# Per-batch feed-forward weights W1 + M1 and W2 + M2 formed in SBUF a turn ahead, in place of correction matmuls in every turn

## The reference

```
lt   = x[:, 1:17];  even, odd = lt[:, ::2], lt[:, 1::2]
m1   = (even[:, :4, :, None] * odd[:, :4, None, :]).reshape(B, 1024, 256)
m2   = (even[:, 4:, :, None] * odd[:, 4:, None, :]).reshape(B, 256, 1024)
h    = gelu(x @ W1.T + scale * x @ m1.T + b1)
out  = h @ W2.T + scale * h @ m2.T + b2
```

## Time and profile before

| | |
|---|---|
| median of three runs | 1988.76 us (1985.94 to 1989.46) |
| profiled execution | 1991.09 us, span 1989.3 us |
| mean granted TensorE clock | 0.995 |
| busy | PE 97%, DVE 69%, ACT 56%, POOL 20% |
| first half, turns 1 to 15 | 63.9 us a turn |
| second half, looped turns | 56.1 us a turn |

### The profile page before, as it was taken

The page is one execution under the profiler, slowest core; times in us unless marked ns, Lnnn a source line. Parts: engine busy times, 40 slices in busy tenths (PEclk is TensorE's granted clock), DMA queues, the critical chain, the costliest instruction groups (busy, mean ns, idle before and its releaser), DMA issues.

```text
span 1989.3 us, 41475 instructions
## 1 busy us (share of the span) xinstructions
PE 1927.2 (97%) x14078; PEld 1803.2 (91%) x14078; DVE 1367.9 (69%) x3408; ACT 1115.5 (56%) x2334; POOL 407.1 (20%) x650
## 2 busy tenths in 40 slices
PE   7999999999999999999987899999999999999998
PEld 6788888888888888888886899999999999999998
DVE  7877776776777776776746566766666666766665
ACT  5655565555655565555655655554555555544553
POOL 2222222222222222222213511111111101111100
PEclk9999999999999999999999999999999999999999
DMA  4000000000000000000012200000000000000000
GB/s 162 12 22 21 11 11 21 21 21 5 16 21 21 11 11 21 21 21 6 10 34 89 67 15 15 12 17 17 11 16 16 17 12 17 12 17 12 17 7 12
DMA packets 47211, 44.51 MB, mean 22 GB/s; under 512 B 6848, under 2 KB 45376, under 8 KB 47168
## 3 DMA queue, kind: packets, MB, share of 16 engines
q1 hardware_dynamic: 47168, 43.96, 6.9%
HBM read 34.77 MB, written 8.39 MB: 22 GB/s over the span
## 4 chain that ended last, share of the span: by engine, by line
PE 83%; DVE 7%; ACT 5%; issue 3%; POOL 1%; SPq 1%; DMA 0%; DVEq 0%; ACTq 0%; POOLq 0%
PE ring L618 9%; PE ring L620 9%; PE ring L619 9%; PE ring L1820 7%; PE ring L1818 7%; PE ring L1819 7%; PE ring L671 4%; PE sim L1818 3%; PE sim L1819 3%; PE sim L1820 3%; PE sim L618 3%; PE sim L620 2%; PE sim L619 2%; PE ps_x L1818 2%; PE ps_x L1820 2%
## 5 line engine op out<-in xcount | busy, mean ns | idle before, releaser
L411 ACT ACTIVATE a_pr<-sim,a_nmax 128x512 f32<-128x512 f32 x256 | 174.5, 689 | 208.4 <-DVE a_nmax L537 208.3
L1818 PE MATMUL ring<-b_xch,b_weh 128*128 128x256 f32 x1024 | 289.5, 283 | 1.7 <-DVE b_act_e L1464 1.7
L1819 PE MATMUL ring<-b_xcl,b_weh 128*128 128x256 f32 x1024 | 285.7, 279 | 0.0
L1820 PE MATMUL ring<-b_xch,b_wel 128*128 128x256 f32 x1024 | 285.6, 279 | 0.0
L326 POOL TENSOR_SCALAR a_pr<-a_pr,a_rinv 128x512 f32<-128x512 f32 x256 | 183.1, 729 | 498.3 <-DVE a_rinv L547 495.4
L1818 PEld LDWEIGHTS ring<-b_xch,b_weh 128*128 128x128 f32 x1024 | 192.3, 188 | 1.9 <-DVE b_act_e L1464 1.9
L1819 PEld LDWEIGHTS ring<-b_xcl,b_weh 128*128 128x128 f32 x1024 | 193.0, 188 | 0.0
L1820 PEld LDWEIGHTS ring<-b_xch,b_wel 128*128 128x128 f32 x1024 | 192.1, 188 | 0.0
L1464 DVE TENSOR_TENSOR b_act_e<-b_act_e,ring 128x512 f32<-128x512 f32 x128 | 87.9, 687 | 116.7 <-PE ring L1820 102.4
L528 DVE TENSOR_TENSOR a_ptl<-ring,a_pth 128x512 fp32r<-128x512 f32 x256 | 163.9, 682 | 3.1 <-ACT a_pth L401 2.0
L515 DVE SCALAR_TENSOR_TENSOR a_ktl<-ring,a_bkv_s,a_kth 128x512 fp32r<-128x512 f32 x128 | 95.3, 744 | 102.1 <-ACT a_kth L391 102.1
(11 more groups left out here) (378 smaller groups left out, 6246.0 us busy)
## 6 DMA issues: line engine op xcount, KB each, us to landing
a_c_in<-in_ctx_in SPq DMA_DIRECT2D x16, 256.0 KB, 2.6
a_x_in<-in_x SPq DMA_DIRECT2D x16, 256.0 KB, 2.9
a_x_res<-in_x SPq DMA_DIRECT2D x16, 256.0 KB, 2.6
x_between<-a_x_out SPq DMA_DIRECT2D x16, 256.0 KB, 2.2
b_x_s<-x_between SPq DMA_DIRECT2D x16, 256.0 KB, 2.6
b_up<-b_ev SPq DMA_DIRECT2D x256, 1.0 KB
out_x<-b_acc SPq DMA_DIRECT2D x16, 256.0 KB, 2.2
b_ct_raw<-in_ctxT SPq DMA_DIRECT2D x15, 256.0 KB, 2.6
```

Source lines behind the costliest of these rows:

```text
L411: nc.scalar.activation(pr[:, h % 2, t, :], sim[t][:], ACT.Exp, bias=nmax[:, h % 2, t:t + 1], accum_out=rsum[:, h % 2, t:t + 1]).then_inc(e ...
L1818: nc.tensor.matmul(out, lh, rh, start=(n == 0), stop=False)
L1819: nc.tensor.matmul(out, lh, rl, start=False, stop=False)
L1820: last = nc.tensor.matmul(out, ll, rh, start=False, stop=(n == len(parts) - 1 and not more))
```

## The change

The corrections are gone. Instead the weights themselves are made for every item, one turn ahead. The item's first 32 rows of `x1` are loaded a second time, normalized apart (`rows_stats`, `rows_rstd`, `rows_apply`), written to DRAM (`rows_between`) and read back in two forms: the eight even rows broadcast to all partitions (`even_b`, 8 KB in each partition) and the odd rows turned (`odd_raw`, single 4-byte elements), by `rows_spread`. ScalarE then writes each rank-one product into the raw weight tiles (`update`, 16 instructions of 128x256 a turn), two accumulating DMAs for each of W1 and W2 (`weights_added`, issued by GpSimd) add the weights from DRAM to them, ScalarE writes the high halves (`weight_high`, eight of 128x512) and GpSimd the low halves (`weight_low`, eight of 128x512). For items 0 and 1 the products are made by GpSimd, in turns 14 and 15 of the first half; turn 14 is written out of the loop for that (`ahead`). The split of W1 and W2 in turn 0 and their load at the start are gone.

Two other things are moved. In each turn the chain's fills stand earlier beside the experts' on TensorE, with VectorE and ScalarE ordered to match. In the warm turn the low halves of experts 4 to 7 go from GpSimd to VectorE.

```diff
+        def rows_spread(n):
+            take(rows_ready, n + 1)
+            sp.dma_start(z_t[n], first_rows[1:1 + 4 * NL, :]).then_inc(rows_out, 16)
+            take(rows_out, n * 16 + 16)
...
+            sp.dma_start(even_b[:], z_two[n, 0].unsqueeze(0).to_broadcast([P, 2 * NL, D])).then_inc(spread_in, 16)
+            for c in range(DC):
+                sp.dma_start(odd_raw[:, c, :], z_two[n, 1][:, c * P:(c + 1) * P].rearrange("r p -> p r"),
+                             allow_slow_non_contiguous=True).then_inc(spread_in, 16)
...
+        def weights_added(n, w):
+            take(w_made[w], n * 4 + 4)
...
+            for c in (slice(0, half), slice(half, 2 * half)):
+                pool.dma_start(dst[:, c], src[:, c], accum_op=ALU.add).then_inc(w_in[w], 16)
+
+        def weight_low(n, w, q):
+            take(w_hi[w], n * 4 + q + 1)
+            raw, high, low = (w_piece(w, q, tile) for tile in W[w])
+            nc.gpsimd.tensor_tensor(low, raw, f32(high), ALU.subtract).then_inc(w_lo[w], 1)
...
     def scalar(act):
+        def update(n, w, q):
+            act.wait_ge(odd_ready, n + 1)
...
+            for k in range(2):
+                part, row, by = rank_one(w, q, k)
+                last = nc.scalar.activation(part, row, ACT.Copy, scale=by)
+            last.then_inc(w_made[w], 1)
+
+        def weight_high(n, w, q):
+            act.wait_ge(w_in[w], n * 32 + 32)
+            raw, high, _ = (w_piece(w, q, tile) for tile in W[w])
+            nc.scalar.activation(high, raw, ACT.Copy).then_inc(w_hi[w], 1)
...
     def tensor(pe):
-                last = nc.tensor.matmul(cd[:, k, :], up1[:, n, k * P:(k + 1) * P], zm[:], start=False, stop=True)
...
                 if chain:
                     pe.wait_ge(lo["A"], t + 1)
-                    pe.wait_ge(lo["Z"], t + 1)
-                    pe.wait_ge(up_in, (t + 1) * UPS * 16)
+                    pe.wait_ge(w_lo["1"], t * 4 + 4)
```

More of the change, by code:

```diff
@@ L296, in turn @@
                 other.early(0)
+            if is_ahead(b):
+                other.ahead(0)
         sections_of(sp, turn)
@@ L357, in turn @@
                     other.early(h)
+                if is_ahead(b):
+                    other.ahead(h)
         sections_of(pool, turn)
@@ L1006, in rest, with turn @@
             sp.sem_inc(out_done, 16)
-            def turn(t, chain, more, warm):
+            def turn(t, chain, more, more2, warm):
+                if more2:
+                    rows_load(t + 2)
                 if more:
@@ L1323, in rest, with turn, experts @@
         def rest():
-            def turn(t, chain, more, warm):
+            def turn(t, chain, more, more2, warm):
                 i = t - 1
-                for e in warm_in(0) if warm else ():
-                    for j in range(3):
-                        expert_high(e, j)
+                def experts(slot):
+                    for e in warm_in(slot) if warm else ():
+                        for j in range(3):
+                            expert_high(e, j)
+                experts(0)
                 silu(i, 1)
@@ L1335, in turn @@
                     gelu_high(t, 1)
-                for e in warm_in(1) if warm else ():
-                    for j in range(3):
-                        expert_high(e, j)
                 if chain:
@@ L1361, in turn @@
-                silu(i, 4)
+                if chain:
+                    copy_high(t, "V", hh[:, V, 0:S])
+                experts(3)
+                if more:
+                    update(t + 1, "1", 2)
                 if chain:
                     copy_high(t, "B", xth[:])
-                    copy_high(t, "V", hh[:, V, 0:S])
+                if more:
+                    update(t + 1, "1", 3)
+                silu(i, 4)
                 hidden_high(i, 4)
-                for e in warm_in(4) if warm else ():
-                    for j in range(3):
-                        expert_high(e, j)
@@ L1396, in turn @@
                     hidden_high(t, 0)
+                if more:
+                    weight_high(t + 1, "2", 2)
+                    weight_high(t + 1, "2", 3)
+                if chain:
                     tanh_high(t)
             sections_of(act, turn)
-        return Beside(early, beside, rest)
+        return Beside(early, ahead, beside, rest)
     def vector(dve):
@@ L1724, in beside, with turn @@
                 distances(0)
+                for q in range(4):
+                    weight_low(1, "2", q)
         def rest():
-            def turn(t, chain, more, warm):
+            def turn(t, chain, more, more2, warm):
                 i = t - 1
@@ L1767, in turn @@
                     norm_apply(t + 1, "A", x1_s)
-                hidden_low(i, 4)
-                weigh(i, 3)
-                if chain:
-                    queries_low(t)
-                hidden(i, 5)
                 if chain:
                     maxima(t)
+                if warm:
+                    for j in range(3):
+                        expert_low(6, j)
+                hidden(i, 5)
                 hidden_low(i, 5)
-                if more:
-                    even_low(t + 1)
                 if chain:
@@ L1819, in product @@
                 nc.tensor.matmul(out, lh, rl, start=False, stop=False)
-                last = nc.tensor.matmul(out, ll, rh, start=False, stop=(n == len(parts) - 1 and not more))
+                last = nc.tensor.matmul(out, ll, rh, start=False, stop=(n == len(parts) - 1))
             return last
```

533 lines of the change are left out of this document (273 added, 260 removed).

## The result

The changed kernel took 2112.32 us (median of four, 2110.63 to 2114.19), the kernel before 1988.72 beside it: ratio 1.062, 95% interval 1.061 to 1.064. The forecast was 1954, with a range to 1998.

The account below looks back on a forecast made before the run. TensorE, busy 97% of the span, was taken as the bound. Net 1.34 us a turn over 14 turns (18.8 us) + 3 + 8 - 1.5 + 7 gave 35 us: 1954 on the median's scale, range 1934 to 1998.

Parts of the forecast that it names:

- What goes from TensorE: Looped turn: update matmuls, narrower `y_fill`, Z, W2 update and G's transposes go, 2.25 us; with B's wait 2.79 us.
- the wait at B: Looped turn, TensorE ahead of B's transposes: the 0.54 us wait goes, as `second_residual` no longer waits for the correction.
- Beside C: Turn's end: C's transposes come before `down` 6, leaving the C chain less time; 0.25 us allowed, bounds 0 and 0.8.
- the GpSimd step: Looped turn: eight low halves on GpSimd, 11.1 us, both weights in time by about 4 and 8 us.
- rival D: Turn's end: GpSimd's low halves lock out an expert's low half, about 1 us a turn, 14 us, 1968; chance 0.12.
- The step on the accumulating DMAs: Looped turn: W1's transfers hidden; W2's land about 10 us after issue, up to 12 allowed: hidden, narrowly.
- The new wait ahead of `y_fill`: Looped turn: two W2 high halves ahead of the tanh delay ScalarE 1.06 us; new wait 1.16, taken as 1.2 us.
- The wait ahead of `o_fill`: Looped turn, TensorE: no wait forecast here; ScalarE's 16 products were taken at 0.4 us each, 6.4 us.
- The landing of the DMAs: Looped turn: W2's accumulating load lands about 10 us after issue, bounds 8.1 and 16.2.
- rival C: W2 DMAs land after their 12 us, ScalarE then TensorE wait; 2037 at 16.2 us; chance 0.18 beyond the sign.
- The single places: Outside the loops: turn 0 gains 3 us, turn 15 gains 8, turn 14 costs 1.5; the warm turn gains 7.
- The warm turn: Warm turn, 66.54 us before: one GpSimd wait goes, VectorE and ScalarE get more work; gain 7, bounds -2 and 12.

Follow-up runs that it names:

- e12: e11 with W1 high halves and W1/W2 low halves spread over the turn, and the routing's last part behind the last gelu low half: 1965.36 us, ratio 0.987.
- e5: Changed kernel with one wait more: GpSimd starts W1's low halves only after VectorE has applied the C norm: 2068.12 us.
- e3: Changed kernel with all four W2 high halves ahead of the R copy on ScalarE: 2059.14 us.
- e1: Changed kernel with C's root on GpSimd between the two accumulating W2 transfers, no longer behind both: 2100.63 us.
- e7: As e6, but the wait on the C norm stands ahead of the second W2 transfer's issue: 2132.48 us.
- e2: Changed kernel without the accumulating transfers (W1 and W2 not added to the products): 2047.86 us.
- e10: e9 with C's root between the W2 transfers, four W2 high halves ahead of the R copy, ScalarE's last two W2 products behind its T copy: 2017.19 us.
- e11: e10 with ScalarE's W1 and W2 products and GpSimd's issue of their transfers earlier in the turn: 1991.01 us, ratio 1.0005 to the kernel before.
- e9: Changed kernel with all eight low halves a turn on VectorE and none on GpSimd: 2059.40 us.
- e8: e7 with e3's order and ScalarE's last two W2 products behind its copy of T: 2094.54 us.
- e6: Changed kernel with e1's root order and e5's wait on the C norm, ahead of the W1 low halves only: 2060.60 us.
- e4: Changed kernel with W2's accumulating transfer in four pieces of 256 KB instead of two of 512 KB: 2158.10 us.

## Why the prediction was wrong

**What goes from TensorE: right in kind, a little too large.** 2.25 us of matmuls and the wait at B were forecast to go. B's wait went. I counted the loops of the kernel before, the changed kernel and e12 from one matmul's start to the next, and call a pause what such a distance has beyond that of matmuls back to back. By this count 1.9 to 2.0 us of matmuls went: `y_fill` got only 0.19 us shorter (48 matmuls in 5.76 us) and not 0.31, and the transposes of G had taken 0.14 us and not 0.21. With the new waits mended (e12) the looped turn is 54.77 us, where 54.8 was forecast. That is luck: e12 has no steady `y_fill` wait where the forecast had 1.2, but besides the waits listed it has short pauses elsewhere. In all it pauses 0.6 us a turn more than the kernel before, for a forecast of 0.9, and lost 0.3 us less of matmuls.

**Beside C: the step that failed.** I allowed 0.25 us, with 0.8 as the most; it was 4.5 us. Two mistakes are in it.

The first is the GpSimd step. I summed its low halves as load, "both are in time", and asked when they are ready, not who runs beside them. The earlier trace rows had the number, and rival D used it once a turn on an expert's low half, 1 us, 14 us in all. The runs put it on two other places, both critical: the C norm (1.9 us a turn; e5 gets 44 us back with one wait) and the routing's two instructions ahead of the gelus (1.62 us; part of e3's 53). The price of one meeting was as I had it, up to one GpSimd instruction; what I had wrong is which instructions meet and how many, four a turn on critical places in the changed kernel. Where I moved the runs, it was at times the whole run: 3.67 us with two (e1), 6.10 with four (e7). The Trainium skill, "SBUF — State Buffer", Who interferes with whom, says that `tensor_scalar` can contend too, in a mode that takes both ports; I had applied the rule to two-input instructions alone. The trace agrees in that the norm and the routing's two, all `tensor_scalar`, were held; the mode itself no trace shows.

The second is the queue. The step on the accumulating DMAs weighed when they land, and the GpSimd step gave issuing them no time. An issue costs GpSimd 1.3 us, and the second half of W2 was not issued until 0.27 us after the first had landed, in every turn, some 6.2 us after the first's issue; C's root was queued behind both. Without transfers (e2) the wait at C fell from 4.5 to 1.6 us. By themselves the root's 3.3 us were worth 12 us (e1), because the norm then met the low halves; with the low halves away they are part of what e10 and e11 gained, a share that no run takes apart.

**The new wait ahead of `y_fill`: right kind, half the size.** The 1.16 us of ScalarE's order are borne out by e9 against e10 (1.2 us); the rest of the 2.5 is the routing, held up.

**The wait ahead of `o_fill`: a term left out, 0.9 us.** ScalarE's W2 products took 748 ns, 0.65 us apart, where the forecast had 0.4 for all sixteen; W1's took 498, 0.4 apart. Four of W2's stand ahead of its copy of T, which comes some 1 us later than with 0.4 each. With those four behind the copy (e8, e10) the wait is gone.

**The landing of the DMAs: nearly right, and rival C not the cause.** I took 10 us for W2, as one transfer, and bounds of 8.1 to 16.2. Each half landed 5.9 us after its issue (W1's 6.9), the two together 12 us after the first issue, because they go one after the other. In the changed kernel no wait of ScalarE for it shows; e6, e7, e8 and e10 met it as soon as C was earlier, with 2.3 to 3.8 us. The Trainium skill, "DMA: Bandwidth & Descriptors", Anatomy of one DMA, gave an estimate of 3.2 us for a 512 KB half; the runs measured 5.9 for one that accumulates.

**The clock: not in the forecast, 3.0 us a turn.** Rival C had priced lower clock behind waits, the forecast had no wait large enough for it. 0.06 of 65.5 us is 3.9 us, some of it while TensorE waited; 3.0 us fell on matmuls. The turn missed 54.8 by 10.7 us, and counted from start to start these are 7.4 us of pauses beyond the forecast's, the 3.0 us of clock, and 0.3 us of matmuls that were to go and didn't.

**The single places.** Turns 0, 14 and 15 were to bring 9.5 us and brought 6.8. The warm turn was to gain 7 and lost 8.3; in e12 it still lost 5.1 (71.6 us), so there VectorE's and ScalarE's added work does not fit. I have not taken it apart. From there to the end 120.7 us were lost where 18.8 were to be gained.

**What the loss was made of, by the runs:** low halves off GpSimd -53 (e9), then the orders of root, high halves and T -42 (e10), the products and transfers earlier -26 (e11), the halves spread -26 (e12). These are steps in this sequence and not independent prices: e3 alone took 53, e5 alone 44.

## What to carry to other kernels

Before moving work to GpSimd, list what VectorE does at that time with inputs from SBUF, and whether TensorE waits for it: here each such instruction was held to the end of one GpSimd instruction (1.35 us in place of 0.41) and in e1, e6 and e7 at times to the end of a whole run, so "GpSimd is 30% busy" says nothing about the price. A wait that keeps GpSimd away from one critical VectorE instruction can be worth more than the work it delays. Ask of a transfer not only when it lands but what is queued behind its issue, above all behind the second of two.

## What the runs showed of the hardware that I had not expected

- Size did not protect a VectorE instruction: one of 128x16 that takes 0.17 us took 0.75 and its neighbour 1.22 beside GpSimd. Behind GpSimd's run of four (5.45 us) one took 6.10 us instead of 0.69 in e7, while in the changed kernel, before its warm turn, three got through during such a run. Instructions with one input in PSUM were not held up: an expert's product (L1560) took 0.69 us beside GpSimd and without it.
- Of transfers issued by GpSimd in 1 KB rows, 512 were outstanding with the next 512 held back (halves), and 768 with the next 256 held back (e4). The issue held back began 0.27 us after the last of the others had landed, and GpSimd could do other work before it (e1). W1's two halves, 1 MB in 256 rows of 4 KB, were issued 0.65 us apart, so it is not a matter of bytes.
- An issue took 1.2 us for 256 KB and 1.3 to 1.4 for 512 KB. An accumulating packet of 1 KB took 102 ns, a plain one 46 (medians).
